# An attention head's output bank joins the ring of score banks: bank, first value product and transpose are moved

## The reference

```python
q, k, v = (to_heads(q), to_heads(k), to_heads(v))
q = apply_rotary(q)
k = apply_rotary(k)
scores = jnp.einsum('bhqd,bhkd->bhqk', q, k) * SCALE
weights = jax.nn.softmax(scores, axis=-1)
attn = jnp.einsum('bhqk,bhkd->bhqd', weights, v)
attn = attn.transpose(0, 2, 1, 3).reshape(B, T, D)
...
x = x + 0.5 * _L0_ffn_ref(_layernorm(x, axis=-1), L0_ffn_Wr, L0_ffn_W1, L0_ffn_W2)
x = x + _L0_attn_ref(_layernorm(x, axis=-1), L0_attn_qkv_w, L0_attn_qkv_b, L0_attn_out_w, L0_attn_out_b)
x = x + 0.5 * _L0_ffn_ref(_layernorm(x, axis=-1), L0_ffn_Wr, L0_ffn_W1, L0_ffn_W2)
```

## Time and profile before

| | us |
|---|---|
| median of 3 runs | 1300.66 |
| lowest and highest of them | 1300.22, 1306.47 |
| the profiled execution | 1300.45 |
| its span, first to last instruction | 1298.7 |
| of it, attention's score maxima (first to last start of L1257) | 358.8 to 974.7 |

### The profile page before, as it was taken

One profiled execution on the slowest core, in us unless ns is written; L12 is line 12 of the kernel. 1 busy time (PEld: TensorE's weight loads), 2 busy tenths in 40 slices (PEclk: granted clock), 3 DMA queues, 4 the chain that ended last, 5 costly groups with the idle time before them and its releaser, 6 DMA issues.

```text
span 1298.7 us, 32041 instructions
## 1 busy us (share of the span) xinstructions
PE 1258.2 (97%) x10240; PEld 613.8 (47%) x10240; DVE 1107.9 (85%) x2306; ACT 807.2 (62%) x1540; POOL 141.7 (11%) x450
## 2 busy tenths in 40 slices
PE   5999999999979999999999999999999999999998
PEld 3666666667622222222222222222223777767776
DVE  7888867887789999999999999999994778777775
ACT  4433333333229999999999999999997333323332
POOL 1020122111221111111111111111110000000000
PEclk9999999999969999999999999999999999999999
DMA  7010111011211111111101011011111000100000
GB/s 211 1 31 19 50 50 41 8 49 50 68 55 33 33 41 31 37 35 31 41 31 41 31 33 39 31 41 31 40 47 32 19 28 28 28 27 25 9 10 9
DMA packets 52265, 48.49 MB, mean 37 GB/s; under 512 B 10080, under 2 KB 44768, under 8 KB 52192
## 3 DMA queue, kind: packets, MB, share of 16 engines
q1 hardware_dynamic: 52192, 47.61, 12.6%
HBM read 23.86 MB, written 23.33 MB: 36 GB/s over the span
## 4 chain that ended last, share of the span: by engine, by line
PE 63%; DVE 29%; issue 7%; DVEq 1%; ACT 0%; DMA 0%; SPq 0%; ACTq 0%
DVE mx L1257 25%; PE ps L780 23%; PE ps L767 16%; PE ps L922 8%; PE ps L909 7%; PE ps L880 2%; PE ps L737 2%; PE ps L757 1%; DVE X L1114 1%; PE ps L701 1%; PE ps L744 1%; DVE act L1102 1%; PE ps L774 1%; DMA w<-w_t 0%; PE ps L719 0%
## 5 line engine op out<-in xcount | busy, mean ns | idle before, releaser
L1257 DVE TENSOR_REDUCE mx<-ps 128x1 f32<-128x1024 f32 x512 | 587.3, 1216 | 22.3 <-PE ps L880 20.9
L676 ACT ACTIVATE probs<-ps 128x512 f32<-128x512 f32 x1024 | 557.3, 601 | 41.9 <-PE ps L909 33.9
L605 ACT ACTIVATE sg<-ps,unscale 128x512 f32<-128x512 f32 x256 | 173.8, 687 | 306.7 <-PE ps L780 285.1
L880 PE MATMUL ps<-K,Q 48*128 48x512 bf16 x1008 | 321.9, 388 | 7.1 <-DVE mx L1257 3.4
L922 PE MATMUL ps<-probs,vh 128*32 128x256 f32 x4096 | 327.8, 392 | 0.0
L909 PE MATMUL ps<-Q,K 51*128 51x512 bf16 x1024 | 319.0, 384 | 0.9 <-ACT probs L676 0.7
L767 PEld LDWEIGHTS ps<-w,act 128*128 128x128 f32 x2048 | 247.9, 192 | 17.1
L767 PE MATMUL ps<-w,act 128*128 128x128 f32 x2048 | 249.0, 275 | 0.0
L1102 DVE SCALAR_TENSOR_TENSOR act<-ps,unscale,sg 128x512 f32<-128x512 f32 x256 | 183.5, 745 | 58.1 <-PE ps L780 18.2
L780 PE MATMUL ps<-x_hi,w_hi 128*128 128x512 f16 x512 | 194.8, 381 | 10.1 <-DVE act L1102 6.2
L1114 DVE SCALAR_TENSOR_TENSOR X<-ps,rw,X 128x128 f32<-128x128 f32 (+1 forms) x512 | 144.0, 344 | 61.7 <-PE ps L767 61.2
(11 more groups left out here) (84 smaller groups left out, 607.9 us busy)
## 6 DMA issues: line engine op xcount, KB each, us to landing
o_parts<-ot SPq DMA_DIRECT2D x64, 128.0 KB, 1.9
q_stack<-parts SPq DMA_DIRECT2D x48, 128.0 KB, 2.3
k_stack<-parts SPq DMA_DIRECT2D x48, 128.0 KB, 2.3
Q<-q_stack SPq DMA_DIRECT2D x64, 96.0 KB, 2.3
K<-k_stack SPq DMA_DIRECT2D x64, 96.0 KB, 2.3
probs<-w_in SPq DMA_DIRECT2D x8, 256.0 KB, 4.7
att<-o_parts SPq DMA_DIRECT2D x16, 128.0 KB, 2.6
rden<-rdens SPq DMA_DIRECT2D x16, 128.0 KB, 2.5
```

The lines of the kernel that those rows point to most:

```text
L605: nc.scalar.activation(sg[:, j, :], hid[2 * j], ACT.Silu, scale=unscale[:, e, 2 + j:3 + j]).then_inc(silu_done, 1)
L676: nc.scalar.activation(probs[:, kb % PSLOTS, j * CH:(j + 1) * CH], score[u][i], ACT.Exp, scale=SCALE).then_inc(probs_ready, 1)
L880: last = nc.tensor.matmul(maxps[t % 2][:, half, :], Q[u][0:STACK, t * P:(t + 1) * P], K[u][0:STACK, half * CH:(half + 1) * CH], start=True ...
L1257: nc.vector.tensor_reduce(mx[:, u % 2, t:t + 1], pair.rearrange("p a b -> p (a b)"), AX_X, ALU.max).then_inc(max_read, 1)
```

## The change

The output bank is no longer a bank of its own. At step 6 (`OUT_AT`) the bank whose turn it is in the ring becomes the output bank of this head, and the output bank of the head before comes into the ring in its place. A table, `Banks`, goes through two turns of four heads and notes for every score, transpose and output which bank it has and who used it last. The names in the diff: `key_user` is the last user of key i's bank, as (what, how many heads back, step), `row_user` that of the transpose, `out_user` that of the output.

With this,
- value 0 goes from step 6 to step 5, and waits for exp 3 (the last user of the bank that it takes) in place of exp 1 and `o_copy`;
- key 6 takes the bank that the head before leaves, and waits for `o_copy` (`ot_ready`) in place of exp 3;
- the transpose goes from before step 7 to before step 8 (`MT_AT` = 8) on PE, and ACT's copy of it from before exp 7 to before exp 8; the very first transpose stays (`FIRST_MT_AT`);
- the transpose's bank was last read by exp 5 (before: exp 4). Behind it the distances read: key 7 waits for exp 4 (before: exp 5), key 8 for exp 6 (as before), key 9 for exp 7 (before: `mrow_copy`), key 10 for `mrow_copy` (before: exp 7), key 11 for exp 8 (as before).

No instruction is added or removed apart from waits. The last head has no transpose; there the table gives key 10 the user of the transpose's bank, exp 5.

```diff
--- before.py
+++ after.py
@@ -59,15 +59,17 @@
 PIECE = H * CH // P
 QSLOTS = 4
 LAG = 2
-FIRST_VALUES = 2 * LAG + 2
 PSLOTS = 8
 HALVES = 2 * KB
 
 
-MT_AT = 7
-SCORE_BANKS = 3
-HEAD_PLACES = HALVES + 1
-PLACES = QSLOTS * HEAD_PLACES + 1
+MT_AT = 8
+FIRST_MT_AT = 7
+OUT_AT = 6
+COPY_AT = 3
+SCORE_BANKS = (0, 1, 2)
+OUT_BANK = 7
+MAX_BANK = 3
 FIRST_PAIRS = 3
 W_OPS = 5
 NEWTON = 3
@@ -80,33 +82,40 @@
     eng.wait_ge(sem, count)
 
 
-def score_place(u, i):
-
-    return HEAD_PLACES * u + i + (i >= MT_AT)
-
-def bank_of(place):
-    return place % SCORE_BANKS
-
-def mt_bank(u):
-    return bank_of(HEAD_PLACES * u + MT_AT)
-
-def place_before(u, place, row):
-
-    n, before = 0, place - SCORE_BANKS
-    if before < 0:
-        n, before = -QSLOTS, before + PLACES
-    if before == PLACES - 1 or (before == HEAD_PLACES * u + MT_AT and not row):
-        before -= SCORE_BANKS
-    n += before // HEAD_PLACES - u
-    at = before % HEAD_PLACES
-    if at == MT_AT:
-        return n, None
-    return n, at - (at > MT_AT)
+class Banks:
+
+    def __init__(self):
+        self.key, self.row, self.out = ([{} for _ in range(QSLOTS)] for _ in range(3))
+        self.key_user, self.row_user, self.out_user = ([{} for _ in range(QSLOTS)] for _ in range(3))
+        ring, out = list(SCORE_BANKS), OUT_BANK
+        user = {}
+        for n in range(2 * QSLOTS):
+            u = n % QSLOTS
+            for i in range(HALVES):
+                if i == OUT_AT:
+                    self.out_user[u] = self.back(user.get(ring[0]), n)
+                    ring[0], out = out, ring[0]
+                    user[ring[0]] = ("out", n - 1, 0)
+                    self.out[u] = out
+                if i == MT_AT:
+                    self.row_user[u] = self.back(user.get(ring[0]), n)
+                    self.row[u] = ring[0]
+                    user[ring[0]] = ("row", n, 0)
+                    ring.append(ring.pop(0))
+                self.key_user[u][i] = self.back(user.get(ring[0]), n)
+                self.key[u][i] = ring[0]
+                user[ring[0]] = ("key", n, i)
+                ring.append(ring.pop(0))
+            if u == QSLOTS - 1:
+                assert tuple(ring) == SCORE_BANKS and out == OUT_BANK, (ring, out)
+
+    @staticmethod
+    def back(last, n):
+        return last and (last[0], last[1] - n, last[2])
+
+BANKS = Banks()
 
 
 class Order:
@@ -241,11 +250,11 @@
         wpsum = [ps[:, 4, :], mpsum_all]
         rpsum = ps[:, 7, 0:TPC * E].rearrange("p (t e) -> p t e", t=TPC)
         vpsum = ps[:, 7, :].rearrange("p (t h d) -> p t h d", t=TPC, h=H)
-        score = [[ps[:, bank_of(score_place(u, i)), :] for i in range(HALVES)] for u in range(QSLOTS)]
-        maxps = [ps[:, SCORE_BANKS + 2 * s:SCORE_BANKS + 2 * s + 2, :] for s in range(2)]
+        score = [[ps[:, BANKS.key[u][i], :] for i in range(HALVES)] for u in range(QSLOTS)]
+        maxps = [ps[:, MAX_BANK + 2 * s:MAX_BANK + 2 * s + 2, :] for s in range(2)]
         first_maxps = [ps[:, 2 * s:2 * s + 2, :] for s in range(FIRST_PAIRS)]
-        mpsum = [ps[0:PARTS * KB, mt_bank(u), 0:P // 2].bitcast(BF16) for u in range(QSLOTS)]
-        opsum = ps[:, 7, 0:QW]
+        mpsum = [ps[0:PARTS * KB, BANKS.row[u], 0:P // 2].bitcast(BF16) for u in range(QSLOTS)]
+        opsum = [ps[:, BANKS.out[u], 0:QW] for u in range(QSLOTS)]
 
 
         expert_loaded = [sem(f"expert_loaded{e}") for e in range(E)]
@@ -661,7 +670,7 @@
 
                 if not (isinstance(r, int) and r == 0 and u < 2):
                     sc.wait_ge(ot_stored[u % 2], 16 * (2 * r + u // 2))
-                nc.scalar.activation(ot[:, u % 2, :], opsum, ACT.Copy).then_inc(ot_ready, 1)
+                nc.scalar.activation(ot[:, u % 2, :], opsum[u], ACT.Copy).then_inc(ot_ready, 1)
 
             def head(r, u, more=True, first=False):
                 n = QSLOTS * r + u
@@ -675,7 +684,7 @@
                         at_least(sc, probs_used, KB * (n - 1) + kb + 1)
                     nc.scalar.activation(probs[:, kb % PSLOTS, j * CH:(j + 1) * CH], score[u][i],
                                          ACT.Exp, scale=SCALE).then_inc(probs_ready, 1)
-                    if i == 3 and not first:
+                    if i == COPY_AT and not first:
                         o_copy(r + (u - 1) // QSLOTS, (u - 1) % QSLOTS)
                     if i == 5 and not more:
                         xT_copy(NCH, 0, early_t)
@@ -882,20 +891,23 @@
                 if half == 1:
                     last.then_inc(max_in_psum, 1)
 
-            def bank_free(n, u, place, row):
-
-                dn, i = place_before(u, place, row)
-                if i is None:
+            def bank_free(n, last):
+
+                what, dn, i = last
+                if what == "key":
+                    at_least(pe, probs_ready, HALVES * (n + dn) + i + 1)
+                elif what == "row":
                     pe.wait_ge(mrow_ready, n + dn + 2)
                 else:
-                    at_least(pe, probs_ready, HALVES * (n + dn) + i + 1)
+                    at_least(pe, ot_ready, n + dn + 1)
 
             def max_transpose(r, u, beside, first=False):
 
                 n = QSLOTS * r + u
                 pe.wait_ge(mparts_ready, n + 1)
                 if not first:
-                    bank_free(n - 1, beside, HEAD_PLACES * beside + MT_AT, True)
+                    bank_free(n - 1, BANKS.row_user[beside])
                 nc.tensor.transpose(mpsum[beside], mparts[:, u % 2, :, :].rearrange("p i t -> p (i t)"),
                                     identb[:]).then_inc(mT_in_psum, 1)
 
@@ -905,7 +917,8 @@
                 kb, j = i // 2, i % 2
                 if i == 0:
                     pe.wait_ge(mrow_loaded[u], 16 * (r + 1))
-                bank_free(n, u, score_place(u, i), row)
+                last = BANKS.key_user[u][i]
+                bank_free(n, BANKS.row_user[u] if last == ("row", 0, 0) and not row else last)
                 nc.tensor.matmul(score[u][i], K[u][0:ROWS, kb * P:(kb + 1) * P],
                                  Q[u][0:ROWS, j * CH:(j + 1) * CH], start=True, stop=True).then_inc(scores_in_psum, 1)
 
@@ -913,13 +926,15 @@
 
 
                 n = QSLOTS * r + u
-                pe.wait_ge(probs_ready, HALVES * n + 2 * kb + 2)
                 if kb == 0:
-
-                    at_least(pe, ot_ready, n)
+                    what, dn, i = BANKS.out_user[u]
+                    assert (what, dn) == ("key", 0) and i >= 1
+                    pe.wait_ge(probs_ready, HALVES * n + i + 1)
                     pe.wait_ge(vh_ready, n + 1)
+                else:
+                    pe.wait_ge(probs_ready, HALVES * n + 2 * kb + 2)
                 for c in range(QUARTERS):
-                    last = nc.tensor.matmul(opsum[VW * c:VW * (c + 1), :], vh[:, u % 2, kb, :],
+                    last = nc.tensor.matmul(opsum[u][VW * c:VW * (c + 1), :], vh[:, u % 2, kb, :],
                                             probs[:, kb % PSLOTS, c * QW:(c + 1) * QW],
                                             start=(kb == 0), stop=(kb == KB - 1), skip_group_check=True)
                 last.then_inc(probs_used, 1)
@@ -927,7 +942,7 @@
             pe.wait_ge(max_read, KB)
             pe.wait_ge(head_loaded[1], 32)
             for i in range(HALVES):
-                if i == MT_AT:
+                if i == FIRST_MT_AT:
                     max_transpose(0, 0, 0, first=True)
                 max_scores(0, 1, i)
 
@@ -944,11 +959,9 @@
                     key_scores(r, u, i, row)
                     if maxes:
                         max_scores(r + (u + 2) // QSLOTS, (u + 2) % QSLOTS, i)
-                    if i == FIRST_VALUES:
-                        weigh_values(r, u, 0)
-                    elif j == 1 and kb > LAG:
+                    if j == 1 and kb >= LAG:
                         weigh_values(r, u, kb - LAG)
-                    elif j == 1 and kb < LAG and not first:
+                    elif j == 1 and not first:
                         weigh_values(r + (u - 1) // QSLOTS, (u - 1) % QSLOTS, KB + kb - LAG)
                     if early == 0 and i == 5:
 
```

## The result

The changed kernel takes 1289.28 us (median of 6 runs, 1285.79 to 1290.57), the kernel before 1301.24 beside it (median of 6, 1300.21 to 1306.47). The ratio is 0.9888, with a 95% interval of 0.9868 to 0.9908: 1.1% faster. The forecast was 1286.8, with a range that took in the 1276 of the first rival and went up to 1291.5. The profiled execution took 1290.57 us with a span of 1288.6, against 1300.45 and 1298.7: 9.9 us less.

The account below looks back on a forecast made before the run. Key 9's lateness behind PE's beat was taken to set the head: 8.86 + 0.34 = 9.20 us against 9.45. Gains of 12.6 + 1.3 - 0.3 sum to 13.6, taking 1300.45 to 1286.8 us; range 1276 to 1291.5.

Parts of the forecast that it names:

- first rival: Key 9 doesn't wait for exp 7; DVE bounds a head at 9.05 us, 1276 us in all; chance 0.13.
- One number, key 9 behind key 4: On PE, key 9's lateness behind its beat of 2.44 us after key 4 adds to 8.86 us a head.
- Value 0 in step 5: On PE, value 0 fills the early gap 0.54 us behind key 4; its wait for exp 3 costs 0 to 0.05.
- Key 6 behind the output copy, and max 6: Copy over at 0.76 us, key 6 at 1.11, so hidden; max 6's 0.46 us wait for DVE goes.
- The transpose for 0.03 us: On PE, the transpose behind value 1 costs 0.03 us; PE alone would reach key 9 at 2.47.
- Key 9 behind exp 7: New wait on PE: exp 7 over at 2.74 us, key 9 at 2.79, a wait of 0.3 us.
- Exps at 0.49 and not 0.52 us: ACT's exps take 0.49 us each back to back; the slower-pace rival with 0.52 gave 1294 us, chance 0.02.
- The loop's jump: PE loses 0.31 us at each four-head turn, now counted in full: 37.1 us a turn against 38.00.
- Everything outside heads 1 to 62: Heads 0 and 63 were counted at nothing in the forecast sum.
- Head 62, counted at -0.3: Without max products nothing waited there for DVE, but key 9 will wait for exp 7: gain of -0.3 us.

Follow-up runs that it names:

- value 0 alone: Kernel before with only value 0 moved from step 6 to step 5, output bank and transpose kept in place: 1305.66 us, ratio 1.0016.
- the changed kernel with the two waits put back: Changed kernel, but in each loop turn's first head key 0 waits for exp 14 and key 1 for exp 15 of the head before: 1289.77 us.

## Why the prediction was right, and where it was not

**One number, key 9 behind key 4.** Right. In every kernel that kept a max tile's halves together, the head was 8.86 us plus what key 9 (or key 11) was late: 9.45, 9.44, 9.43, 9.32, 9.20, 9.12 and 9.10 measured. With value 2 between the halves PE's lateness set it no longer, DVE's did, 9.49.

**Value 0 in step 5.** Right: 0.53 behind key 4, no cost, as the row of key 6 had said. The part that the output bank plays in it was shown by value 0 alone, which had to wait until 0.85.

**Key 6 behind the output copy, and max 6.** Right: key 6 at 1.10, max 6 beside it.

**The transpose for 0.03 us.** Right where it stands in the change, behind a value. As a price of its own it was not: 0.25 between two keys, shown by value 0 alone, where exp 5 was over in time. With the exchange and the transpose in its old place it would lie hidden in the wait for exp 5, so that run can't show it.

**Key 9 behind exp 7.** Right: 2.79 forecast, 2.77 measured, and exps 4 to 7 over at 2.71, 0.03 before the forecast. Outside the loop, where even exps start 0.08 earlier, a head takes 9.12.

**Exps at 0.49 and not 0.52 us.** The four exps took 2.08 us; at a pace of 0.49 the last of them is over 0.61 + 3 x 0.49 = 2.08 behind the start of the first, at 0.52 it would be 2.17. The trace agrees within 0.01 with the page "Perfetto Trace Analysis" of the Trainium skill, section Optimizing Scalar/DVE Operations, whose 51 ns of overhead on PSUM make an estimate of 0.48, and not with the 0.52 worked out from the Trainium skill's page "ScalarE: Activation LUTs", section What ACT_TABLE_LOAD costs.

**The loop's jump.** Wrong, and this is the step that was mis-sized. I read 0.31 us in the earlier trace rows as the price of the jump, and argued that it would count in full once PE set the pace: 4 x 9.20 + 0.31 = 37.1. They were waits for exps 14 and 15, from the place that the ring left unused at the end of a turn, and the change takes that place away: in its table the banks are back in their first order after each turn, with no place left over. A turn was 36.84, 1.16 less than before and not 0.90, so the 14 turns gave 16.3 us instead of 12.6. The rows could have told it: exp 15 is over 0.05 before key 1, the same 0.05 by which I had recognised exp 3 ahead of key 6.

**Everything outside heads 1 to 62.** I counted it at nothing; it cost 7.9 us in the profiled execution. How much of that is the clock, the record of the changed kernel with the two waits put back tells: it has the clock of the record of before (mean 0.989, at 1.2 GHz from 357.5 for 6.8 us and from 371.2 for 20.5), and there the part outside heads 1 to 62 is only 0.6 longer than before (0.1 ahead of head 1, 0.3 in the last head, 0.2 behind it). Its span is 1285.9; without the 4.5 us of the two waits that is 17.3 less than before. So, by one execution of each, the change is worth some 17 us at equal clock, and 7.3 of the 7.9 are the clock's. The two misses are of opposite sign, 4.3 more gain and 7.9 less, and that 1286.8 came near 1289.3 is luck: the length of a head was right, the sum around it was not. Without the second, the sum would have been 1300.45 - 17.9 = 1282.5. Head 62, counted at -0.3, came at -0.1 (10.05 to 10.16 us).

## What to carry to other kernels

When several engines are each nearly full, find the one event per turn at which the beat is broken, and say what it waits for; the head's length follows from it, and each edit can be priced by how far it moves that event. A gap at a loop's jump is not the jump's own price until the waits of its first instructions have been followed one by one: buffers that rotate with a period that doesn't divide the turn put a tighter dependence exactly there. Filling an engine's wait with other work helps only if what follows is not thereby late for a third engine.

A forecast of the total can land by two errors that cancel. Compare the part that the change touches by itself, at the same clock, before calling the sum right.

## What the runs showed of the hardware

The order of two waits on ACT is worth time, and which order is the better one depends on where the code stands. In the loop, an exp starts 0.50 us behind its key product with the wait that is long over placed behind the one that ends last, and 0.42 with it placed ahead. In heads 1 to 3, outside the loop, where the thresholds are constants, it is the other way round: 0.42 with it behind and 0.48 with it ahead.

A transpose of 128 x 24 costs PE 0.03 us behind a value product, which uses all 128 rows, and 0.25 between two key products, which use 51. Whether the rows are the reason was not tested.

With the same instructions on PE, the granted clock fell to 1.2 GHz for 3.4 us at about 35 us in some executions and not in others, and for 7 to 10 us in the last attention head in some; among runs of one kernel the time goes with the mean clock, by 0.5 us (1286.17 at 0.986, 1288.11 at 0.982) to 1 us (1285.79 at 0.987, 1290.57 at 0.982) for 0.001. PE at work for 9.40 of 10 us did not prevent it. What decides it was not found.
